# One program for experts and attention, with GpSimd taking the low parts of q and k of the first row half

## What is computed

```python
x = x + _L0_ffn_ref(_L0_cond_ref(cond_2048, x, ...), ...)     # recurrence, then 2 of 8 experts
x = x + _L1_ffn_ref(_L1_cond_ref(x, cond_2048[:, None, :], ...), ...)
# _L1_cond_ref:
xn = _rms_norm(x, g_norm) * (1.0 + scale) + shift
q, k, v = split(xn @ W_qkv)                  # 16 heads of 32
q = _rms_norm(q, g_q)
k = _rms_norm(k, g_k)
logits = einsum('bhqd,bhkd->bhqk', q, k) * d ** (-0.5)
o = einsum('bhqk,bhkd->bhqd', softmax(logits), v)
return o + o @ W_out
```

## Time and profile before

| what | us |
|---|---|
| median of 3 runs | 1751.67 |
| the profiled execution | 1755.36 |
| its span, first to last instruction | 1753.6 |
| TensorE busy | 1566.3 (89%) |
| VectorE busy | 1188.7 (68%) |
| ScalarE busy | 901.8 (51%) |
| GpSimd busy | 617.0 (35%) |

### The profile page before, as it was taken

The page is one execution under the profiler, slowest core; times in us unless marked ns, Lnnn a source line. Parts: engine busy times, 40 slices in busy tenths (PEclk is TensorE's granted clock), DMA queues, the critical chain, the costliest instruction groups (busy, mean ns, idle before and its releaser), DMA issues. The chain is left out here.

```text
span 1753.6 us, 76408 instructions
## 1 busy us (share of the span) xinstructions
PE 1566.3 (89%) x31935; PEld 1213.6 (69%) x31935; DVE 1188.7 (68%) x4281; ACT 901.8 (51%) x3325; POOL 617.0 (35%) x1831
## 2 busy tenths in 40 slices
PE   6999999999999999999469975788889887799999
PEld 5999999999999999998346642455556555444444
DVE  5778788787877888887665536677767667573231
ACT  5555555555555555654425544467767777431130
POOL 0333333333333333333345534243333444570000
PEclk8999999999999999855579997899889998899999
DMA  4110101101110011110627534000000010120001
GB/s 176 50 27 11 46 25 29 41 15 54 41 38 5 23 48 47 40 29 16 210 80 246 181 104 143 25 26 1 1 1 1 1 55 2 55 91 24 25 0 49
DMA packets 45736, 91.28 MB, mean 52 GB/s; under 512 B 6609, under 2 KB 25169, under 8 KB 45393
## 3 DMA queue, kind: packets, MB, share of 16 engines
q1 hardware_dynamic: 39152, 65.94, 11.8%
q0 software_dynamic: 6240, 20.45, 3.5%
HBM read 67.69 MB, written 18.61 MB: 49 GB/s over the span
## 5 line engine op out<-in xcount | busy, mean ns | idle before, releaser
L412 PE MATMUL bank<-arena 128*128 128x8 f16 x12288 | 502.5, 170 | 10.0 <-issue 5.0
L415 PE MATMUL bank<-arena 128*128 128x16 f16 x12288 | 497.9, 182 | 3.0 <-issue 2.1
L412 PEld LDWEIGHTS bank<-arena 128*128 128x128 f16 x12288 | 412.8, 97 | 38.8 <-ACT bank L509 18.4
L415 PEld LDWEIGHTS bank<-arena 128*128 128x128 f16 x12288 | 412.6, 97 | 5.8 <-issue 4.5
L676 POOL TENSOR_TENSOR arena<-arena 128x16 f32<-128x16 f32 x512 | 117.8, 230 | 535.4 <-DVE arena L619 521.3
L479 ACT ACTIVATE arena<-arena 128x16 f32<-128x16 f32 x512 | 114.8, 224 | 307.9 <-DVE arena L598 307.5
L609 DVE TENSOR_TENSOR_SCAN arena<-arena,bank 128x64 f32<-128x64 f32 x512 | 146.9, 287 | 18.9 <-ACT arena L479 2.3
L598 DVE TENSOR_REDUCE arena<-bank 128x16 f32<-128x48 f32 x512 | 100.4, 196 | 86.9 <-PE bank L415 81.3
L2064 PE MATMUL bank<-arena 128*128 128x512 f16 x704 | 152.3, 379 | 1.7 <-PEq L1416 1.7
L385 PE MATMUL bank<-arena 128*128 128x256 f16 x1008 | 147.0, 272 | 1.1 <-issue 1.0
L1474 PE MATMUL bank<-arena 128*128 128x512 f16 x576 | 138.3, 392 | 5.0 <-DVE arena L1812 5.0
(11 more groups left out here) (207 smaller groups left out, 2683.7 us busy)
## 6 DMA issues: line engine op xcount, KB each, us to landing
arena<-yrows SPq DMA_DIRECT2D x16, 512.0 KB, 3.9
arena<-in_wgu SPq DMA_DIRECT2D x48, 128.0 KB, 2.3
arena<-in_wdn SPq DMA_DIRECT2D x8, 512.0 KB, 4.0
hrows<-arena SPq DMA_DIRECT2D x16, 256.0 KB, 3.8
arena<-in_xtok SPq DMA_DIRECT2D x16, 256.0 KB
out_y<-arena SPq DMA_DIRECT2D x16, 256.0 KB, 2.0
arena<-in_wih SPq DMA_DIRECT2D x4, 768.0 KB, 7.4
arena<-in_whh SPq DMA_DIRECT2D x4, 768.0 KB, 10.5
```

The source lines that it names most:

```text
L412: mm = nc.tensor.matmul(dst[:, j * B:(j + 1) * B, 1], w, h[:, 0], start=home not in opened, stop=False, skip_group_check=True)
L415: mm = nc.tensor.matmul(dst[:, j * B:(j + 1) * B, 1:3], w, h.rearrange("p a c -> p c a"), start=home not in opened, stop=False, skip_group ...
```

## The change

1. The experts' and attention's blocks become one; the engines no longer meet between them. The experts' output buffer is moved (`ye` in place of `yo`) so that attention's first tiles don't lie on it, and VectorE waits for `y_evac` before it begins.
2. `EARLY` is 4 where it was 6. So the lists before the first batch hold two groups fewer, and batches 0 to 5 turn two groups each (before: 0 to 4). The sums and residuals of the sixth and seventh group (6 and 7) move into batch 0, and so on by one batch.
3. `unit_rows` for a batch's groups stands at heads 11 and 12 of the batch before, not at heads 0 and 1 of its own.
4. The sums of groups 0 and 1 are VectorE's (`first_sum`), and ScalarE does `adaptive`'s work for group 1 (`turned`).
5. `low_qk` of i = 0 and 1 of each sequence but the first stands in GpSimd's list behind the four `squares`, and no longer in VectorE's at head 5.
6. In ScalarE's loop `high_o2` stands ahead of `stack`, not behind it.

```diff
-        yo = m.take([3, D], F32)
+        ye = Mem(arena, raw_top - 4 * 4 * D).take([3, D], F32)
...
-        with nc.Block() as block:
...
-        EARLY = 6
+        EARLY = 4
...
-        LOW_AT = {5: (0, 1), 6: (2, 3)}
+        LOW_AT = {6: (2, 3)}
...
 # TensorE, before the first batch
                 turn_back(2)
-                turn_back(3)
                 project(0, 1, True)
-                turn_back(4)
-                project(0, 2, True)
-                turn_back(5)
-                for i in range(3, 6):
+                turn_back(3)
+                for i in range(2, 6):
                     project(0, i, True)
...
 # ScalarE
+                def turned(g):
+                    b, half = divmod(g, 2)
+                    act.wait_ge(turn_mm, g + 1)
+                    for k in range(KT):
+                        op = A.activation(xnf[:, b, k, half * P:(half + 1) * P], turn_bank(g)[:, k * P:(k + 1) * P],
+                                          ACT.Identity, scale=ada[:, 0, k, b:b + 1], bias=ada[:, 1, k, b:b + 1])
+                    op.then_inc(xnf_done, 1)
...
                         if h + 1 < H:
                             softmax(b, h + 1)
+                        if 11 <= h < 11 + len(turned_in(b + 1)):
+                            unit_rows(turned_in(b + 1)[h - 11])
...
-                            if h < len(turned_in(b)):
-                                unit_rows(turned_in(b)[h])
...
-                            for g in STACK_AT.get(h, ()):
-                                stack(b + 1, g)
                         if b > 0:
                             for jp in O2_AT.get(h, ()):
                                 high_o2(b - 1, jp)
+                        if not last:
+                            for g in STACK_AT.get(h, ()):
+                                stack(b + 1, g)
...
 # VectorE
+                def first_sum(g):
+                    dve.wait_ge(yb_in[g], 16)
+                    V.tensor_tensor(ysum[:, g, :], yb[:, g, 0, :], yb[:, g, 1, :], ALU.add).then_inc(ysum_done, 1)
...
+                dve.wait_ge(y_evac, TILES)
...
 # GpSimd
+                def low_qk(b, i):
+                    lo, again = (1, 2) if i % 2 == 0 else (2, 1)
+                    pool.wait_ge(qk_hi, 4 * b + i + 1)
+                    G.tensor_copy(stk[:, i, :, again * DH:(again + 1) * DH], stk[:, i, :, 0:DH])
+                    G.tensor_tensor(stk[:, i, :, lo * DH:(lo + 1) * DH], heads_of(qkr[:, i, :]), stk[:, i, :, 0:DH],
+                                    ALU.subtract).then_inc(qk_lo, 1)
...
                         for i in range(4):
                             squares(b + 1, i)
+                        low_qk(b + 1, 0)
+                        low_qk(b + 1, 1)
```

More of the change, by code:

```diff
@@ new lines, in _ @@
+                turn_back(0)
+                turn_back(1)
+                project(0, 0, True)
+                turn_back(2)
+                project(0, 1, True)
+                turn_back(3)
+                for i in range(2, 6):
+                    project(0, i, True)
+                for g in range(4):
+                    stack(0, g)
+                pe.wait_ge(xnf_done, EARLY)
+                for h in range(H):
+                    scores(0, h, True)
+                pe.wait_ge(vzero, 3)
@@ L952, in _ @@
+                turn_max(0)
+                project(1, 0)
+                scores_t(0, 0, True)
+                scores_t(0, 1, True)
+                for b in range(B - 1):
+                    batch(b, False)
+                batch(B - 1, True)
             @block.scalar
@@ new lines, in _ @@
+                A.activation(mxs[:, 0, 0:1], epsb[:, :], ACT.Sqrt)
+                for g in range(2):
+                    square_rows(g)
+                    root_rows(g)
+                unit_rows(0)
+                unit_rows(1)
+                turned(1)
+                norm_x(0, 0)
+                norm_x(0, 1)
+                for g in (2, 3):
+                    square_rows(g)
+                    root_rows(g)
+                unit_rows(2)
+                unit_rows(3)
+                take_out(0, 0)
@@ new lines, in _ @@
+                take_out(0, 1)
+                for g in (4, 5):
+                    square_rows(g)
+                    root_rows(g)
+                take_out(0, 2)
+                take_out(0, 3)
+                root(0)
+                take_out(0, 4)
+                take_out(0, 5)
+                for n in range(4):
+                    high_qk(0, n)
+                norm_x(1, 0)
+                norm_x(1, 1)
+                for g in range(4):
+                    stack(0, g)
+                turn_max(0)
@@ L1023, in _ @@
+                high_v(0)
+                for g in turned_in(0):
+                    unit_rows(g)
+                for b in range(B - 2):
+                    batch(b, False, True)
+                batch(B - 2, False, False)
+                batch(B - 1, True, False)
             @block.vector
```

899 lines of the change are left out of this document (412 added, 487 removed).

## The result

The changed kernel takes 1721.84 us (median of 4 runs, 1719.34 to 1725.52). Beside it on the same chip the kernel before takes 1749.24 (4 runs, 1744.05 to 1752.48). The ratio is 0.9848, 95% interval 0.9815 to 0.9881: faster by 27.4 us. The forecast was 12.9 us faster, 1739, with a range from 1726.

A forecast was written before the change was run, and what follows sets the result against it. TensorE was taken to bound attention, with about 10 us a batch of idle time to win. The seven terms sum to -12.9 us, from the median 1751.67 to 1738.8, say 1739; range 1726 to 1751.

The forecast's parts named there:

- Terms 1 to 3: Start of attention: joined blocks -6.4 us, `turned` on ScalarE -1.0, two groups fewer ahead of the first batch -2.2.
- Term 4: Batches 4 and 5: the two groups moved inside the batches add one step to each, +5.5 us.
- Term 5: Batches: early `unit_rows` removes TensorE's waits ahead of `turn_back`, -8.2 us, but lengthens the end of the batch before, +2.8.
- Term 6: Six batches: `high_o2` ahead of `stack` brings TensorE's second stack sooner, 1.85 us a batch, -11.1 us.
- Term 7: Seven batches: half of `low_qk` on GpSimd frees nothing; contention with VectorE delays the first stack 1.1 us each, +7.7 us.
- GpSimd for nothing: Rival, chance 0.20: GpSimd's share of `low_qk` costs nothing, so the +7.7 us falls away, 1731 us.
- The gain caught again: Rival, chance 0.17: VectorE's maxima and take-outs behind the second stack bind the batch's tail, cancelling `high_o2`'s gain, 1750 us.
- the late GpSimd: Rival, chance 0.05: GpSimd's four `low_qk` instructions average 3.5 us and release the first stack 6.1 us late, 1774 us.

The follow-up runs named there:

- early6: Changed kernel with six groups turned and eight summed ahead of the first batch, all sums on GpSimd, `turned` on VectorE alone; ratio to the kernel before 0.985.
- units_late: Changed kernel with `unit_rows` of each batch's groups back at its own heads 0 and 1; ratio to the kernel before 0.9872.
- before_low_pool: Kernel before with one edit: `low_qk` of tiles 0 and 1 done by GpSimd; ratio to the kernel before 1.0009.
- low_back: Changed kernel with `low_qk` of tiles 0 and 1 back on VectorE at head 5; ratio to the kernel before 0.9835.
- before_o2_ahead: Kernel before with one edit: ScalarE does `high_o2` ahead of `stack`; ratio to the kernel before 0.9912.
- join_alone: Kernel before with only the experts' and attention's blocks joined; ratio to the kernel before 0.9968.

## Why the prediction was wrong in size

Terms against measurements, in us. The rests are single profiles; the two executions of the changed kernel differ by 1.4, and a slow first projection in one batch more or less is 1.3 to 1.7.

| term | forecast | measured |
| --- | --- | --- |
| 1 to 3, the start | -9.6 | -11.6 and -12.5 (to the first `turn_max`) |
| 4, groups in batches 4 and 5 | +5.5 | +5.55 (early6), of it 1.7 a slow projection |
| 5, units early | -5.4 | -5.4 (units_late) |
| 6, high_o2 ahead | -11.1 | -15.0 (alone), -16 (undone) |
| 7, low parts on GpSimd | +7.7 | +2.1 (alone), +3.5 (undone; 0 by its timing) |
| sum | -12.9 | -23 to -26; measured whole -26.1 and -27.5 |

The parts don't add up to better than some 4 us: the expectation of early6 had 688.6 for its rest by adding the single parts, and it measured 684.5. Both numbers for term 7 hold mostly shifts of the clock in first projections (see before_low_pool and low_back); its own lateness of 0.3 us a batch makes 1 to 2 us.

**Term 7 is the step that failed**, and term 6 the one that was sized too small. In term 7 I forecast that the first stack comes 1.1 us later in each of 7 batches; before_low_pool shows 0.2 to 0.3 in batches 1 to 4 and nothing in 5 and 6. I costed what goes from VectorE at nothing, since VectorE would only wait longer, and then charged the contention (2.6 us on the normalisations, of which 1.1 was to reach the stack) against no slack at all. The same slack was meant in both: the contention is 1.70 us in the normalisations and 0.95 in `low_p` of 6, together 2.65; of that 1.60 goes into the time freed and 0.64 into VectorE's own wait, both in the rows of low_back, which leaves 0.4 against the 0.32 measured. And I passed on lateness from all three normalisations (ScalarE about 1.2 late), though only the first had a waiter in rows 6; ahead of the next two ScalarE has some 1.8 us of softmax and take-out, which cover them. What passes is 0.32. GpSimd's prices were not the trouble: the subtraction takes 1.60 beside VectorE and the copy 0.61 or 1.07, where I took 1.15 and 0.9 alone; the four take 4.76 us instead of 4.1. The same overlap that I feared is there; it had no waiter. The Trainium skill (SBUF — State Buffer, Who interferes with whom) was right on which instructions it hits, the normalisations too: 3.59 us against 1.89. My forecast had hung too much on it: that an instruction blocks does not say that anybody waits for it.

**Term 6 is a true mechanism with too small a price**, -11.1 for a measured -15.0. I took 1.85 us from batch 1's rows for all six batches (the recorded "1204.63 - 2.78" stands for 1204.63 - 1202.78), which leaves a distance of 2.15; it became 1.80. And batch 1 has the distance 4.00 before, batches 2 and 3 have 4.57 and 4.85, and the tail's matmuls run at a higher clock once the waits are gone. Nothing in rows 6 contradicted that; the windows by batch would have shown it (tails of 21.0 to 21.85 us in batches 1 to 3, granted clock 0.84 to 0.74). Batch 0, my control, has a slow clock too: in before_o2_ahead its tail takes 18.7 us at 0.85, that of batch 1 18.05 at 0.91.

**Term 5 came out by luck.** The waits are gone (none ahead of `turn_back` is left in any batch), and the price in the tail is small (0.3 to 0.4 us in batches 0, 1 and 4, none in 2 and 3, where I took 0.55). But in batches 1, 2 and 5 most of the gain is eaten by the clock behind `turn_max`, 1.6 to 1.7 us each, which no term had.

**Terms 1 to 3 were right in kind and somewhat small.** The load leaves 2.8 us behind the scatter (forecast 3), and join_alone alone brings the first sum 5.6 us forward (forecast 5.5); the start is 2 to 3 us shorter than I had it, 0.7 of this ahead of the first transposes (-7.1 for -6.4), 0.3 behind them to the projection (-1.3 for -1.0) and 1.1 from there to the first stack (-3.3 for -2.2). Term 4 hit its number by luck (see early6).

**The rivals.** GpSimd for nothing (1731, 0.20) was the nearest to what came, but not by its reason: the contention is there. The gain caught again fell with before_o2_ahead, the late GpSimd with before_low_pool. The range's low end, 1726, was set a little beyond that rival, and no end of a term allowed for the clock: even the far end of term 6 (-12.6) was the price of one place times six.

**What stays open.** Why the granted clock falls behind `turn_max` in batches 1, 2 and 5 of the changed kernel and not in 3 and 4 is not known: neither the units in the tail nor TensorE's busy time in the last 4.76 us decides it. Why batch 0's first projection takes 4.15 us in the kernel before and 3.99 to 5.33 in the others is not explained either. How much of a difference between two variants is such a shift of the clock can be read only from the projections, batch by batch. Of the start's parts, `turned` on ScalarE and the sums on VectorE weren't tried singly.

## What to carry to other kernels

Charge contention only where the delayed instruction has a waiter in the trace, and set it against the slack that the same move frees. If a wait recurs in every stage, read it in every stage, with the clock beside it: here the tails with the longer waits also had the lower granted clock, so a wait cost its own length and slower matmuls beside it. When an argument says that an instruction standing in line "holds" something, try the swap: moving `low_qk` ahead of `low_p` of head 7 was worth more than giving half of it to another engine, and by the rests it made that gift a loss.

## What the hardware showed that I had not expected

- TensorE's tails: the same 222 matmuls took 17.61 us at a granted clock of 0.74, 16.40 at 0.84 and 15.00 at 0.91. Twelve matmuls of a projection take 2.75 us at the full clock (2.4 GHz), and 4.35 us where the stretch has 0.61. Both came right behind 4.76 us in which TensorE was busy for 3.08, in batch 3 and in batch 1 of the same execution.
- GpSimd and VectorE take turns on both sides: beside each other VectorE's three normalisations take 3.59 us instead of 1.89, GpSimd's copy 1.07 instead of 0.61 and its subtraction 1.60, where its `low_p` of the same shape takes 1.15.
- VectorE's copy of 128x512 between 2-byte tiles takes 0.29 us and GpSimd's 0.61 at best. So giving that copy away frees less on VectorE than it costs on GpSimd.
